# Moving a PSUM copy ahead of the previous step's work in the first phase of a linear-attention and FFN kernel

## What is computed

```python
xn = layernorm(x)                                  # over the 2048 columns
q, k, v = xn @ Wq.T + bq, xn @ Wk.T + bk, xn @ Wv.T + bv
sq, sk = elu(q) + 1, elu(k) + 1                    # k and v: 4 heads, each shared by 4 of q
kv   = einsum('bhsd,bhse->bhde', sk, v)            # summed over all 4096 rows of a batch
attn = (sq @ kv) / (sq . sk.sum(rows) + 1e-6)
s    = attn @ Wo.T
h    = relu((xn @ sign(up).T) * up_scale)
g    = silu((h @ sign(down).T) * down_scale * output_scale)
return x + s * g
```

## Time and profile before

| | |
|---|---|
| time, median of 11 runs | 3978.72 us (3967.52 to 4150.19) |
| time of the profiled execution | 3972.06 us |
| span of the profiled core (core 0, the slowest) | 3970.2 us |
| spans of the eight cores | 3941.5 to 3970.2 us |
| TensorE matmul busy | 2946.5 us (74%) |
| ScalarE / VectorE / GpSimd busy | 705.2 / 536.4 / 240.4 us |
| mean granted TensorE clock, per core | 0.894 to 0.903 |

### The profile page before, as it was taken

How to read it: one execution, slowest core, us unless ns; L and a number is a source line. 1 busy time by engine, 2 the same in 40 slices (tenths; PEclk the granted TensorE clock), 3 DMA queues, 4 the chain that set the end, 5 groups by cost and what they waited for, 6 DMA issues and landing times.

```text
span 3970.2 us, 34895 instructions; the slowest of 8 cores (3941.5 to 3970.2 us)
## 1 busy us (share of the span) xinstructions
PE 2946.5 (74%) x13190; PEld 1311.4 (33%) x13326; DVE 536.4 (14%) x870; ACT 705.2 (18%) x982; POOL 240.4 (6%) x454
## 2 busy tenths in 40 slices
PE   3666676867755558669888696698887867988975
PEld 1333322622211123226333232353332324433332
DVE  2444421011111120210000102100001021000011
ACT  1222223222221110321110003211100032111000
POOL 0000000001011110001110000011100000111000
PEclk9888888899987779879999998799998978999988
DMA  5768411599999984124334641234346313333443
GB/s 128 179 166 226 140 48 48 128 185 195 190 220 205 208 203 147 58 70 133 130 124 130 199 122 53 86 124 132 128 131 192 120 48 104 127 128 127 134 146 111
DMA packets 170178, 543.42 MB, mean 137 GB/s; under 512 B 16112, under 2 KB 16144, under 8 KB 159520
## 3 DMA queue, kind: packets, MB, share of 16 engines
q0 software_dynamic: 59744, 239.16, 26.3%
q1 hardware_dynamic: 79168, 201.35, 17.1%
q10 hardware_dynamic: 31104, 100.68, 6.9%
HBM read 520.15 MB, written 109.05 MB: 158 GB/s over the span
## 4 chain that ended last, share of the span: by engine, by line
PE 44%; DMA 27%; ACT 6%; issue 5%; DVE 3%; ACTq 0%; DVEq 0%; SPq 0%; POOL 0%; POOLq 0%
PE psc L810 17%; DMA dn_sl<-dnS 12%; PE psc L958 10%; PE psc L601 8%; DMA dnS<-dn_sl 7%; PE psc L735 5%; DMA up_sl<-upS 5%; DMA upS<-up_sl 2%; PE psc L667 2%; PE psc L912 2%; ACT up_sl L779 1%; DMA y<-yt 1%; ACT r_tmp L655 1%; ACT r_row L659 1%; ACT qb L611 1%
## 5 line engine op out<-in xcount | busy, mean ns | idle before, releaser
L810 PE MATMUL psc<-xn_t,up_sl 128*128 128x512 bf16 x4096 | 935.5, 385 | 200.6 <-ACT up_sl L779 91.1
L958 PE MATMUL psc<-dn_sl,hidden 128*128 128x512 bf16 x3009 | 701.6, 388 | 130.2 <-DMA dn_sl<-dnS 99.1
L810 PEld LDWEIGHTS psc<-xn_t,up_sl 128*128 128x128 bf16 x4096 | 391.5, 99 | 743.3 <-issue 322.1
L958 PEld LDWEIGHTS psc<-dn_sl,hidden 128*128 128x128 bf16 x3072 | 295.8, 99 | 535.9 <-issue 222.2
L816 ACT ACTIVATE hidden<-psc,uscb 128x512 bf16<-128x512 f32 x256 | 175.9, 687 | 902.9 <-PE psc L810 902.9
L601 PE MATMUL psc<-xn_t,wq_sl 128*128 128x512 bf16 x1024 | 329.6, 495 | 5.3 <-DVE t_all L1023 3.6
L868 PE MATMUL psc<-dn_sl,hidden 128*128 128x512 bf16 x501 | 165.8, 491 | 160.9 <-ACT dn_sl L845 102.4
L1023 DVE TENSOR_TENSOR t_all<-psc,dsb 128x512 f32<-128x512 f32 x64 | 39.0, 681 | 1789.8 <-PE psc L958 1668.0
L735 PE MATMUL psc<-wo_sl,attn_t 128*128 128x256 bf16 x2048 | 240.6, 283 | 32.9 <-ACT s_tile L745 22.6
L392 PE MATMUL ps_k<-wkb,xn_fm 128*128 128x512 bf16 x480 | 168.7, 527 | 124.0 <-DVE xn_fm L380 123.7
L667 PE MATMUL psc<-r_row,ones_r 1*128 1x512 f32 x128 | 91.3, 800 | 202.2 <-ACT r_row L659 202.2
(11 more groups left out here) (81 smaller groups left out, 1323.8 us busy)
## 6 DMA issues: line engine op xcount, KB each, us to landing
dn_sl<-dnS SPq DMA_DIRECT2D x224, 512.0 KB, 3.8
up_sl<-upS POOLq DMA_DIRECT2D x192, 512.0 KB, 3.6
wq_sl<-wqS SPq DMA_DIRECT2D x64, 512.0 KB, 3.3
wo_sl<-woS POOLq DMA_DIRECT2D x32, 1024.0 KB, 5.4
t_all<-up_pre POOLq DMA_DIRECT2D x64, 512.0 KB, 8.7
upS<-up_sl ACTq DMA_DIRECT2D x64, 512.0 KB, 6.1
t_all<-dn_pre POOLq DMA_DIRECT2D x64, 512.0 KB, 10.6
dnS<-dn_sl ACTq DMA_DIRECT2D x64, 512.0 KB, 8.4
```

What stands on the lines that cost most here:

```text
L810: OP("tensor", lambda e, dc=dc, w=up_sl[usl], p=pu: e.matmul(p[:, :], w[:, dc * 128:(dc + 1) * 128], xn_re[:, :, dc, :], start=(dc == 0), ...
L958: ntd=ntd, b=bank, d=dn_sl[dsl]: e.matmul(PS[b][:, :], hidden[:, j * 512 + sub * 128: j * 512 + (sub + 1) * 128], d[:, j2 * 1024 + ntd * 5 ...
```

## The change

The copy of `ps_tr` to `xn_fm` and the store of `xn_fm` are taken out of `body_kv` into a function of their own, `emit_evac`, and are emitted directly behind the transposes of the same step. So the copy of step `st + 1` stands ahead of the VectorE work on k and v of step `st`, where before it stood behind that and behind the layernorm of step `st + 3`. No instruction is added or taken away, and the buffers stay the same.

```diff
-        def body_kv(st):
+        def emit_evac(st):
             own = st < NSUB_OWN
             tau, sub = st // 4, st % 4
             sl = st % NS
-            psl = st % 2
             W("vector", S["PE"], rec["pe_tr"][st])
             if st >= NS:
                 W("vector", S["PE"], rec["pe_v"][st - NS])
...
                 xw_done[st] = S[f"XW{st % 4}"].v
+
+        def body_kv(st):
+            own = st < NSUB_OWN
+            tau, sub = st // 4, st % 4
+            sl = st % NS
+            psl = st % 2
             W("tensor", S["VE"], rec["ve_tre"][st])
...
         body_tr(0)
+        emit_evac(0)
         for st in range(NSUB):
             if st + 1 < NSUB:
                 body_tr(st + 1)
+                emit_evac(st + 1)
             body_kv(st)
             if st + 3 < NSUB:
                 emit_ln(st + 3)
```

## The result

The changed kernel's median is 3892.09 us over 12 runs (3876.05 to 4122.63), against 3980.6 us for the kernel before. The ratio of the two is 0.9767, with a 95% interval of 0.9748 to 0.9786: 93 us of 3980 saved, with 85 to 100 as the interval. The forecast was 3903 us, with 3862 to 3948 as its range.

The account below looks back on a forecast made before the run. Phase A was taken as bound by TensorE waiting for the copy behind the layernorm. Core 0 saves 23 + 20 + 37 - 2 = 78 us; 75 off the slowest gives 3897, plus 6.7 for the median 3903 us, range 3862 to 3948.

Parts of the forecast that it names:

- The wait of k for the copy goes, and the layernorm is what it stood behind: Phase A, TensorE: the 123.7 us wait for xn_fm, whose copy stood behind the layernorm on VectorE, disappears.
- VectorE has room: Phase A: VectorE's own chain takes 8.6 us a turn, below TensorE's 9.26 us, so kb isn't late.
- The own rows: First 15 turns: a loop of 5.76 us plus 8.0 us load landing binds; core 0 saves 23 us.
- The start: Beginning of phase A: load 3 is issued some 1.5 us later than before; 2 us allowed as loss.
- The Wo turns: Eight turns while Wo tiles pass: DMA binds at 12.9 us a turn, saving 20 us, between 0 and 27.
- The last six turns: Last turns with a layernorm: fall to TensorE's 9.26 us, saving 37 us, or 23 at 11.5 us a turn.
- Sum: Whole kernel: core 0 saves 78 us; 75 us taken off the slowest core, giving 3903 us for the median.
- A: Phase A: loads don't bind, nearly all 29 turns reach 9.26 us; 178 us less, 3801; half form, about 3850, 0.10.
- B: Phase A: landings stretch, only the last six turns gain, 23 to 37 us; median 3942 to 3956; chance 0.13.
- C: Denser phase A sets off the 0.81 clock, lasting into phase C; held 500 us, +40, near 4019; chance 0.04.
- D: Phase A: the copy's own conditions hold it, so it isn't earlier in effect; no change, 3979; chance 0.03.
- The signs named beforehand: Phase A profile: own-row turns 13.9 us, wrong under 12 or above 15; last turns 9.3 at clock 1.00; end near 467.

Follow-up runs that it names:

- run 3: Kernel before, with 16 matmuls of 512 columns, results overwritten, added per turn to fill TensorE's wait for the copy; ratio 0.9869.
- run 1: Changed kernel with the store of xn_fm put back in body_kv, so only the copy is moved; ratio 0.9697 to the kernel before.
- run 5: Changed kernel with the own rows' store and load issued after sk_t instead of after the copy; ratio 0.9903 to the kernel before.
- run 8: Kernel before, with the own rows' store and the load behind it also waiting for xn_tm of step st+2; ratio 1.0019.
- run 9: Kernel of run 5 with no weight tile before turn 16; own-row turns 14.9 us, profiled execution 3946.09 us, no ratio.
- run 10: Changed kernel with 26 matmuls of 512 columns, results overwritten, added per turn; 3961.3 us in one execution, beside 3980.48 us.
- run 7: The changed kernel measured again without edits, beside run 5 and run 6; ratio 0.9683 to the kernel before.
- run 6: Changed kernel with the store back in body_kv and the 24 weight tiles spread over the turns; median 3807.66 us, ratio 0.9545.

## Why the prediction was right, point by point

- **The wait of k for the copy goes, and the layernorm is what it stood behind**: right, 123.7 us to 0.8. The price behind the gap was read from the earlier trace rows and is shown by run 3, at 2.2 us a turn.
- **VectorE has room**: right. In the last turns nothing of it shows, and the turn is 9.23 us, as in the earlier trace rows.
- **The own rows**: the mechanism was right, as runs 1 and 5 show, and so was its 5.76 us. The mis-sized term is the landing, "I take 8.0, since the store, the load and the weight tile's transfers keep their order against each other". They kept their order, and the landing still fell to 6.2 to 6.9 us. Why it fell stays open (runs 8 to 10). Nor is the store ahead in the queue the main reason for 8.0 us where a lone load took 4.8: with the store and no weight tile, run 9 has 5.5 to 6.0 us. The forecast gave core 0 23 us and a core like core 7 only 4; they saved 52.0 and 41.1, and the average was 43.4. The lower bound of 7.5 us for the landing was the shortest of one core's loads with work beside it, and core 2's median was below it already (6.9 us): the bound should have been taken over all cores.
- **The start**, -2 us: wrong and small. The first `v_t` comes at 79.0 us on the average, before and after, and the first turn is 9.2 to 9.5 us on all cores, so the later issue of the first load cost nothing.
- **The Wo turns**: 12.8 us for the forecast 12.9, 20.5 us saved for 20, and DMA at 0.94 in this stretch. ScalarE's wait for tiles is the path that was named for it.
- **The last six turns**: 32.8 us for 37. Six cores settled at 9.2 us; cores 4 and 5 ran 10.9 us at 0.81, as bounded by the earlier trace rows. The Trainium skill's rule (TensorE: Matmul & The Clock Gate, section Seeing it yourself) is that a die goes to 13/16 once a third core on it runs dense matmuls. The level is there, but the trace doesn't agree on the condition: cores 6 and 7, of the same die, ran the same turns in 9.2 us and never showed it, and no core of run 10 left the upper level in a TensorE-bound phase A. In run 7 all four cores of this die did show it, in turns that the load bound.
- **Sum**: 78 us were forecast for core 0. Its last `v_t` came 106 us earlier, and that of the average core 98; 75 were forecast for the slowest, and the ratio says 93. Of the 20 us between 78 and 98, the own rows, where the landing was mis-sized, give all (43.4 for 23); the smaller errors, -4 in the last six turns and +4 in the start and the last two, cancel. The 3892 us beside 3903 look closer than the terms were: phase C took 8 us more in the profiled execution, and the allowance for the slowest core is a guess.
- **The rivals**: A (all turns at TensorE's 9.2 us) needs the loop cut and the tiles spread; run 6 shows that even then the Wo turns stay at 10.9. The argument against it, 10.8 us of DMA a turn, was not sound. The kernel before moved 15.4 us x 167 GB/s = 2.6 MB a turn, and the changed one as much, 12.9 x 199, in 0.69 x 12.9 = 8.9 us of busy DMA. The busy share of an unhurried stretch is not the time that its bytes need. B (landings stretch as turns shorten) went the other way. C (the clock) came in its small form: cores 4 and 5 took some 13 us longer than the others for the last eight turns, where they had lost some 8 us before the change. (The prediction counts seven of eight mean clocks above 0.89; with 0.894 as the lowest, all eight were.) D fell with the waits.
- **The signs named beforehand**: the own-row turns are 12.5 us on the average, inside 12 to 15, but core 0's own are 11.96, just under; and the last turns ran at 0.81 on two cores of eight. Phase A ends near 448 us, not 467. The clock in the own rows, expected to be no better, rose from 0.83 or 0.84 to between 0.89 and 0.92.

## What to carry to other kernels

When a wait is removed, look for the closed loop that has the next least slack: add up one round of it from one event back to the same event, and set it against the turn that is hoped for. Here, that sum named the new bound before the run, and moving one transfer's issue off the loop was worth nearly as much again in those turns (36 us) as the change itself (43 us). A landing time isn't a property of a transfer: take its range over all cores, and expect it to move with what is issued ahead of it and, as here, when the turn gets shorter.

## What was not expected of the hardware

- Sixteen useless matmuls of 512 columns a turn, put into a wait of 4.2 us, made the kernel 1.3% faster.
- The same 1 MB load with a 0.5 MB store ahead of it landed after 5.5 to 6.0 us with no weight tile in flight (run 9), and after 9.3 to 10.3 with one issued ahead of it (run 5). With one issued behind it, it took 6.2 to 6.9 us in the changed kernel's turns of 12.5 us and 6.9 to 9.2 in the turns of 15.4 us before.
- The granted clock of 0.81 came and went in both cores of a pair together, twice with the other pair of the die joining (in runs 7 and 8), and not in other executions of equal or denser work: all eight cores ran run 6's own rows without it.
